# A two-layer decoder on one core: norm statistics ahead of two divisions, two exponentials ahead of the router's evictions, and the gate maximum turned two units sooner

## The reference

```
x = x + linear_attention(layernorm(x))        # elu+1 features, running sums, division by the sum
x = x + cross_attention(layernorm(x), ctx)    # 77 keys, softmax
x = x + experts(layernorm(x))                 # router: logits, top 2 of 16, capacity 640
x = x + latent_attention(layernorm(x))
x = x + cross_attention(layernorm(x), ctx)
x = x + feed_forward(layernorm(x))
```

```
x    = act_qdq(x)                     # scale = max|x| / 32767, round, clip, scale back
up   = act_qdq(x @ w_up.T)
gate = act_qdq(x @ w_gate.T)          # needs the maximum over every token first
sig  = fixed_qdq_u16(sigmoid(gate))
gate = act_qdq(gate * sig)
out  = act_qdq(gate * up) @ w_down.T
```

## Time and profile before

| | |
|---|---|
| times of three runs | 1778.44, 1782.88, 1787.87 us (median 1782.88) |
| profiled execution | 1775.84 us, its span 1774.1 us |
| mean granted TensorE clock | 0.942 |
| PE / DVE / ACT / POOL busy in the span | 87% / 54% / 46% / 26% |
| first phase (`layer0`) | up to about 606 us |
| feed-forward | from 1436.67 us |

### The profile page before, as it was taken

The page is one execution under the profiler, slowest core; times in us unless marked ns, Lnnn a source line. Parts: engine busy times, 40 slices in busy tenths (PEclk is TensorE's granted clock), DMA queues, the critical chain, the costliest instruction groups (busy, mean ns, idle before and its releaser), DMA issues. The chain is left out here.

```text
span 1774.1 us, 26885 instructions
## 1 busy us (share of the span) xinstructions
PE 1552.3 (87%) x10059; PEld 1077.1 (61%) x10059; DVE 957.2 (54%) x2226; ACT 827.6 (47%) x1820; POOL 459.4 (26%) x582
## 2 busy tenths in 40 slices
PE   6999999998887399999996999999999879993099
PEld 3666766666665177787873666666666634441088
DVE  3565667756765343222214565566655445599932
ACT  4445564564464122212113556656656423596740
POOL 3222233343434300000006554454333200131000
PEclk9999999999998699999997999999999979997599
DMA  3430101011211144435343101110000000000211
GB/s 109 148 146 17 44 28 52 24 38 53 87 50 51 65 157 122 146 107 158 94 134 93 43 25 40 41 53 30 10 17 16 13 12 1 0 1 6 89 36 60
DMA packets 99680, 107.12 MB, mean 60 GB/s; under 512 B 25314, under 2 KB 88556, under 8 KB 99552
## 3 DMA queue, kind: packets, MB, share of 16 engines
q1 hardware_dynamic: 93408, 88.83, 16.1%
q0 software_dynamic: 6144, 16.57, 2.9%
HBM read 63.59 MB, written 42.01 MB: 60 GB/s over the span
## 5 line engine op out<-in xcount | busy, mean ns | idle before, releaser
L1876 ACT ACTIVATE c_pr<-bank,c_nmax 128x256 f32<-128x256 f32 x256 | 117.9, 474 | 151.1 <-DVE c_nmax L1957 132.0
L1629 POOL TENSOR_SCALAR c_pr<-c_pr,c_rsum 128x256 f32<-128x256 f32 x256 | 127.8, 514 | 224.0 <-DVE c_rsum L1962 223.8
L1396 ACT ACTIVATE b_G<-bank 128x320 f32<-128x320 f32 x128 | 56.0, 437 | 209.7 <-PE bank L1346 209.7
L1346 PE MATMUL bank<-b_XT,shared 128*128 128x320 f32 x512 | 153.5, 434 | 0.0
L1360 PE MATMUL bank<-shared,b_G 128*128 128x256 f32 x640 | 142.2, 379 | 0.0
L1360 PEld LDWEIGHTS bank<-shared,b_G 128*128 128x128 f32 x640 | 120.9, 190 | 17.8
L954 DVE TENSOR_TENSOR a_A<-bank,a_causal 128x512 f32<-128x512 f32 x128 | 79.4, 683 | 71.0 <-PE bank L480 70.9
L1957 DVE TENSOR_REDUCE c_nmax<-bank 128x2 f32<-128x512 f32 x128 | 82.2, 683 | 55.0 <-PE bank L1668 54.2
L415 POOL TENSOR_TENSOR a_L<-a_L,a_Lm 128x1232 f32<-128x1232 f32 x32 | 71.9, 2248 | 147.4 <-DVE a_Lm L969 147.4
L1346 PEld LDWEIGHTS bank<-b_XT,shared 128*128 128x128 f32 x512 | 91.8, 191 | 27.1 <-issue 0.4
L1415 DVE COPY b_Y<-bank 128x256 f32<-128x256 f32 x80 | 33.9, 424 | 120.3 <-PE bank L1360 120.1
(11 more groups left out here) (315 smaller groups left out, 3434.3 us busy)
## 6 DMA issues: line engine op xcount, KB each, us to landing
shared<-L_ffn_w SPq DMA_DIRECT2D x32, 512.0 KB, 6.2
t_slots_in<-a_h SPq DMA_DIRECT2D x20, 512.0 KB, 6.9
shared<-t_slots_in SPq DMA_DIRECT2D x15, 640.0 KB, 7.1
t_slots_out<-b_Y SPq DMA_DIRECT2D x15, 640.0 KB, 4.1
a_xin<-x SPq DMA_DIRECT2D x8, 512.0 KB, 3.8
a_xr<-x SPq DMA_DIRECT2D x8, 512.0 KB, 3.9
t_x_a<-hT_all SPq DMA_DIRECT2D x8, 512.0 KB, 2.9
shared<-t_x_a SPq DMA_DIRECT2D x8, 512.0 KB
```

Of the source, the lines that this page charges most:

```text
L1346: t = p.matmul(P[2 + n % 2][:, 0:HC], w1[e % 3][:, u, 128 * f:128 * f + 128], XT[e % 2][:, u, HC * m:HC * m + HC], start=(u == 0), stop=(u ...
L1629: p.tensor_scalar(pr[k][:, e, u, :], pr[k][:, e, u, :], rsum[k][:, e, u:u + 1], 1.0, ALU.mult, ALU.mult).then_inc(q.pr_ready, 1)
L1876: a.activation(pr[t % 2][:, e, u, :], P[e][:, S * u:S * u + S], ACT.Exp, bias=nmax[t % 2][:, e, u:u + 1], accum_out=sums[t % 2][:, e, u:u ...
```

## The change

Four moves, with no arithmetic altered:

```
 ACT, step 4                                ACT, step 6
+if back2: exponents(g - 2, 1)             +if back2: exponents(g - 2, 2)
 if back4: keep("logits", g - 4, ...)       if back4: (wait for top) a_prob = exp(-top)
-if back2: exponents(g - 2, 1)             -if back2: exponents(g - 2, 2)
```

```
 DVE, step 3
-if back3: divide("xtok2", ...); divide("xtok3", ...)
 if back1: wait for proj0, proj1; moments(1, g - 1, ...)
+if back3: divide("xtok2", ...); divide("xtok3", ...)
 if ahead2: shifts(0, g + 2)
```

```
 PE, feed-forward, within the loop over the up units
-if m == 3:
+if m == 1:
     p.wait_ge(q.bank_free, NU - 3)
     turn_max("g")
-if m == 4:
+if m == 2:
     spread_peak("g")
```

```
 ACT, feed-forward, behind the 48 evictions of the gates
-for m in range(4):
+a.activation(gi[2][:, 0:1], inv["x"][:, :], ACT.Sigmoid)
+for m in range(2):
     keep_up(m)
 a.wait_ge(q.scaled, 2)
 gate_int(0)
+keep_up(2)
+sigmoid(0)
 gate_int(1)
-sigmoid(0)
+keep_up(3)
```

More of the change, by code:

```diff
@@ L903, in _ @@
                             keep_columns("xcol1", g - 3, axT, 1)
+                        if back2:
+                            exponents(g - 2, 1)
                         if back4:
                             keep("logits", g - 4, lgT[:, :], bank("logits", g - 4)[0:E, :])
-                        if back2:
-                            exponents(g - 2, 1)
                     if s == 5:
@@ L921, in _ @@
                             keep_norm(0, g + 2, hT0)
+                        if back2:
+                            exponents(g - 2, 2)
                         if back4:
@@ L924, in _ @@
                             a.activation(prob[:, :, :], top[:, :, 0:TOPK].rearrange("p j k -> p k j"), ACT.Exp, scale=-1.0).then_inc(q.eneg, 1)
-                        if back2:
-                            exponents(g - 2, 2)
                     if s == 7:
@@ L1112, in _ @@
                     if s == 3:
-                        if back3:
-                            divide("xtok2", g - 3, 2, xrden, q.xden_ready, xat)
-                            divide("xtok3", g - 3, 3, xrden, q.xden_ready, xat)
                         if back1:
@@ L1119, in _ @@
                             moments(1, g - 1, x1[(g - 1) % 3])
+                        if back3:
+                            divide("xtok2", g - 3, 2, xrden, q.xden_ready, xat)
+                            divide("xtok3", g - 3, 3, xrden, q.xden_ready, xat)
                         if ahead2:
```

## The result

| | before | changed |
|---|---|---|
| median, us (13 runs each) | 1782.88 (1778.44 to 1787.87) | 1775.62 (1769.12 to 1780.43) |
| ratio, 95% interval | | 0.9955 [0.9942, 0.9969] |
| profiled execution, us | 1775.84 | 1778.07 |
| its span, granted clock | 1774.1, 0.942 | 1776.3, 0.935 |

The change makes the kernel 0.45% faster, 8.0 us (5.5 to 10.3). The ratio is estimated over all runs of both kernels; the two medians lie 7.3 us apart. The forecast was 1776.3, 0.37% faster and "same" by the bound of 0.5%.

What follows compares the result with a forecast made beforehand. PE bounds the first phase; in the feed-forward PE leads until the gate's maximum is turned, then DVE. Terms -5.0 (feed-forward) and -1.5 (first phase) give -6.5 us: 1776.3 against the median 1782.88, range 1770 to 1784.

Steps and rivals of the forecast that it cites:

- The turn: Feed-forward: PE turns the gate's maximum behind two up units instead of four; first `gate_int` 3.43 us sooner, PE losing nothing.
- ACT's order: Feed-forward: `gate_int` to DVE's first product 4.84 us instead of 5.90, table load moved under cover, `keep_up(3)` the late one.
- first rival: Feed-forward: ACT's order keeps the product back, only the turn's 3.4 us stay, first phase gains nothing; 1779.5 us, chance 0.2.
- The end of the tiles: Feed-forward: the earlier start lasts through DVE's tiles, 4.5 + 0.5 = 5.0 us gained; bounds 3.4 to 5.9.
- PE's wait of 4.10: Feed-forward, before PE's last two units: the wait for a magnitude goes, and PE is late by under half a microsecond.
- Step 3: First phase: statistics ahead of divisions hold `xv` 0.34 us at g = 4 to 7 (+1.4 total), about 1.3 at g = 8.
- The collision at L1002: Step 3, g = 3 to 5: L1002 meets POOL's subtraction; the 2 us wait is just covered, taken as 0.
- Step 4: First phase, g = 4 to 7: exponential ahead of logits' eviction removes PE's 0.24 us wait, 4 x 0.24 = -1.0 us.
- Drain: g = 8 and 9: PE's 1.94 us wait exchanged for 1.3 (-0.7); the 1.06 wait at g = 9 goes (-1.0).
- step 6: First phase, ACT: the moved instruction was only 0.1 us long, so -0.1 twice.
- The first phase: Sum of steps 3, 4, 6 and the drain: -1.5 us, bounds -4.2 to +2.7.
- The slower rival: Step 3: divisions become the bound, statistics' 1.91 us show in PE at g = 3 to 8, +11.5; 1787.5 us, chance 0.05.

Runs made afterwards that it cites:

- The 2 x 2 of runs: Kernel before with the feed-forward's turn alone, ACT's order alone, or both: ratios 1.0005, 0.9997 and 0.9973; the fourth case is the kernel before.
- The run without a stretched product: Kernel before with both feed-forward parts (turn and spread earlier, ACT's new order with early sigmoid), first phase unchanged: 0.9973, median 1768.35 us.
- the three runs of the same code: Three kernels with neither the exponentials' nor the statistics' move: 18.9 us from the transposes at g = 8 to the router's count, 18.0 in the profile of before.
- the second: The changed kernel run once more, beside three variants on the same chip, against the kernel before: 0.9940 [0.9919, 0.9962], 6 runs, median 1773.72 us.

## Why the prediction was right

- **The turn**: 3.43 us forecast, 3.43 measured (`gate_int` at 6.16 instead of 9.59), and PE lost nothing.
- **ACT's order**: 4.84 from `gate_int` to product forecast, 4.83 measured, with `keep_up(3)` as the late one, as said. The table load ran under cover.
- **That the two add up** was right as a sum (4.50) and wrong as a reason. The prediction spoke of the turn's 3.4 as its own, and its first rival kept 3.4 if the order gave nothing. The 2 x 2 of runs shows 1.44 and 1.06 apart: the turn could only come through because the new order took `keep_up(3)` from in front of `gate_int(0)`. I had not looked for what stands ahead of the instruction that becomes ready sooner.
- **The end of the tiles**: 5.0 forecast. By rows: 4.50, and 0.52 for DVE's wait that is gone, less 0.61 for a second product that POOL stretches, makes 4.41; measured 4.45. The run without a stretched product gives 4.50 + 0.52 + 0.84 = 5.86; measured 5.91, which is also what PE's end gives (89.12 - 83.18 = 5.94), the upper bound of the prediction. This collision was missed; the prediction had seen the same pair only in step 3.
- **PE's wait of 4.10** is gone, as said, and the last units ran without a gap.
- **Step 3**: 0.34 forecast for L598 at g = 4 to 7, 0.31 measured; 1.3 at g = 8, 1.03 measured. The collision at L1002 came in g = 3 to 5 and was covered, as said; the run with the shifts first shows it.
- **Step 4**: 0.24 forecast for each of g = 4 to 7, 0.40 measured: the mis-sized term. I took the wait itself, while the transposes behind it (L574) and L581 gained too. The net of a group is -0.09 instead of +0.10.
- **Drain**: -0.7 forecast at g = 8, -0.75 measured against the profile of before, but -1.6 against the three runs of the same code whose clock fell behind the wait; -1.0 at g = 9, -1.12 measured (L608 at 551.14 without a wait). At step 6 -0.2 was forecast and nothing is left: the two waits of step 7 are 0.1 and 0.2 shorter, and the next ones in PE's list are longer by about as much. The prediction put all seven waits of the earlier trace rows in g = 8 and 9; the largest one is at g = 10, and the change does not touch it.

The first phase so gains 4 x 0.09 + 0.75 + 1.12 = 2.2 instead of 1.5, or 3.1 with the usual clock at g = 8. With 4.5 to 5.9 of the feed-forward that is 6.7 to 9.0 us, inside the first measured interval (5.5 to 10.3) and from the low end of the second (6.8 to 14.4) upwards. That the forecast of 6.5 came so near is in part luck: half a microsecond too much in the feed-forward stood against 0.7 or more too little in the first phase. The slower rival (PE bound by the divisions) decided nowhere: at g = 4 to 7 DVE's wait of 1.26 hid most of the statistics, as the prediction argued.

## What to carry to other kernels

When a result is made ready sooner, look at what stands ahead of its user in that engine's own list: the gain ends at the next in-order wait, and two edits that each measure as nothing may be one edit in two halves. A wait of PE is worth more than its length where the clock falls behind it, so price it from several runs and not from the one profile at hand. Follow a shortened wait to the next wait of the same engine before you count it: the 0.2 us of step 7 came back there in full. And compare kernels by distances around the change, since the same stretch of the program took 70.7 to 80.6 us from one profile to another.

## What the hardware showed that I had not expected

- With DVE's two-input product and POOL's conversion starting 0.07 us apart, either can be the one that is stretched (2.04 against 1.22, or 2.19 against 1.05), with the same lists of the feed-forward; on DVE's side it costs 0.84 us of path.
- Behind a wait of PE of 1.94 us in the drain the clock fell in six profiles of seven and behind 0 to 1.06 us in none of seven.
- The table load with a one-column activation behind it cost 1.40 us to the start of `keep_up(0)` (1533.25 to 1534.65; the load itself is 1.28), with no further drain seen. The Trainium skill ("ScalarE: Activation LUTs", What ACT_TABLE_LOAD costs) counts 1.38 us more; these rows do not show it.
